# A mamba block and a mixture of experts on one core: the order of the first four and last six sequences written out by instance, and blank rows stored in long runs

## The reference, cut to what matters

```python
# layer 1, for each sequence
xn = layernorm(layernorm(x)) * norm_w + norm_b
x_in, z = split(xn @ in_proj_w.T)                  # 256 channels each
u = silu(conv4(x_in) + conv_b)                     # dense convolution over time, 4 taps
delta_s, B, C = split(u @ x_proj_w.T)              # 1, 16 and 16 columns
delta = softplus(delta_s @ dt_w.T + dt_b)
h[t] = h[t-1] * exp(-delta[t]) + B[t] * u[t]       # recurrence over 512 steps
y[t] = h[t] . C[t]
a = (y * silu(z)) @ out_proj_w.T + residual
x = x + layernorm(a)
# layer 2, over all 8192 tokens
logits = layernorm(x) @ Wr + br                    # 16 experts, the best 2 per token
e_out = layernorm((silu(x W1) * (x W3)) W2) * gamma + beta
x = x + layernorm(w0 * e_out0 + w1 * e_out1)
```

## Time and profile before

| what | us |
|---|---|
| median of 3 runs | 969.74 (968.95 to 969.86) |
| the profiled execution: its own time | 971.61 |
| its span on the core | 969.8 |
| stage 1, to the matmul of the slot columns (L2086) | 0 to 498.8 |
| hand-off, to the first transpose of stage 2 (L2098) | 498.8 to 516.2 |
| stage 2 with the final sums | 516.2 to 969.8 |

### The profile page before, as it was taken

The page is one execution under the profiler, slowest core; times in us unless marked ns, Lnnn a source line. Parts: engine busy times, 40 slices in busy tenths (PEclk is TensorE's granted clock), DMA queues, the critical chain, the costliest instruction groups (busy, mean ns, idle before and its releaser), DMA issues.

```text
span 969.8 us, 26624 instructions
## 1 busy us (share of the span) xinstructions
PE 936.2 (97%) x7189; PEld 829.9 (86%) x7189; DVE 724.0 (75%) x2524; ACT 687.8 (71%) x1355; POOL 619.7 (64%) x814
## 2 busy tenths in 40 slices
PE   8999999999999999998986999999999999999995
PEld 4777877888878877887986999999999999999962
DVE  2379999999999998898832676776777767777747
ACT  3777787777787787774215777777787777877626
POOL 2345677777777777775561666666666666576647
PEclk9999999999999999999997999999999999999998
DMA  4001332221112111111794311111111111111076
GB/s 136 12 12 34 91 96 69 67 78 53 55 56 50 55 40 42 42 22 41 262 310 160 101 44 52 48 52 46 50 50 46 49 50 46 45 52 48 20 274 246
DMA packets 54160, 75.25 MB, mean 78 GB/s; under 512 B 11104, under 2 KB 32866, under 8 KB 53377
## 3 DMA queue, kind: packets, MB, share of 16 engines
q1 hardware_dynamic: 42640, 54.61, 18.5%
q0 software_dynamic: 8672, 16.93, 5.0%
q10 hardware_dynamic: 2704, 2.02, 0.8%
HBM read 47.09 MB, written 27.41 MB: 77 GB/s over the span
## 4 chain that ended last, share of the span: by engine, by line
PE 78%; DVE 7%; POOL 6%; issue 4%; DMA 3%; SPq 1%; ACT 1%; POOLq 0%; DVEq 0%; ACTq 0%
PE pA L2106 11%; PE pR L2106 11%; PE pA L1665 11%; PE pB L2114 6%; PE pY L2114 5%; PE pY L1779 4%; PE pB L1691 3%; PE pB L1825 3%; PE pA L1680 3%; PE pY L1815 3%; POOL chosen_scratch L698 3%; PE pY L1798 2%; PE pY L1747 2%; PE pR L1763 2%; POOL ers L688 1%
## 5 line engine op out<-in xcount | busy, mean ns | idle before, releaser
L698 POOL DMA_INDIRECT chosen_scratch<-yo,got_id x143 | 147.8, 1034 | 94.0 <-issue 88.1
L1026 ACT ACTIVATE stage<-w_sb 128x1024 f32 x143 | 151.2, 1057 | 59.1 <-issue 37.6
L1545 DVE TENSOR_TENSOR hidT<-pR,sil 128x512 f32<-128x512 f32 x143 | 98.9, 692 | 89.7 <-ACT sil L1021 60.9
L612 POOL DMA_INDIRECT slots_scratch<-xrow,send_at x128 | 134.2, 1049 | 34.3 <-issue 30.4
L2106 PE MATMUL pA<-xsT,stage 128*128 128x128 f32 x1144 | 153.0, 277 | 0.4 <-ACT xsT L1010 0.4
L2106 PE MATMUL pR<-xsT,stage 128*128 128x128 f32 x1144 | 152.1, 276 | 0.0
L2106 PEld LDWEIGHTS pA<-xsT,stage 128*128 128x128 f32 x1144 | 140.9, 194 | 0.7 <-ACT xsT L1010 0.7
L2106 PEld LDWEIGHTS pR<-xsT,stage 128*128 128x128 f32 x1144 | 140.1, 193 | 0.0
L1665 PE MATMUL pA<-xn,taps 128*128 128x512 f32 x256 | 129.8, 593 | 1.0 <-DVE taps L1062 1.0
L688 POOL TENSOR_TENSOR ers<-eve,neg_half 128x1 f32<-128x1 f32 x143 | 81.3, 569 | 58.1 <-DVE eve L1557 56.8
L1021 ACT ACTIVATE sil<-pA 128x512 f32<-128x512 f32 x143 | 85.3, 596 | 28.2 <-PE pA L2106 26.2
(11 more groups left out here) (233 smaller groups left out, 2099.7 us busy)
## 6 DMA issues: line engine op xcount, KB each, us to landing
got<-slots_scratch SPq DMA_DIRECT2D x143, 65.0 KB, 1.9
w_sb<-chosen_scratch SPq DMA_DIRECT2D x16, 512.0 KB, 5.3
w_sb<-in_w_dram SPq DMA_DIRECT2D x1, 6144.0 KB, 19.1
xin<-in_x_dram SPq DMA_DIRECT2D x16, 256.0 KB, 3.9
xr<-in_x_dram SPq DMA_DIRECT2D x16, 256.0 KB, 3.1
x_scratch<-x SPq DMA_DIRECT2D x16, 256.0 KB, 3.7
w_sb<-in_w_dram SPq DMA_DIRECT2D x4, 1024.0 KB, 7.8
fx<-x_scratch SPq DMA_DIRECT2D x1, 4096.0 KB, 14.5
```

Source lines behind the costliest of these rows:

```text
L612: eng.indirect_dma_start(slots_d, bass.IndirectOffsetOnAxis(ap=send_at[:, s % 2, k, t:t + 1], axis=0), xrow[:, s % 2, k, t, :], None).then ...
L698: eng.indirect_dma_start(chosen_d, bass.IndirectOffsetOnAxis(ap=got_id[:, j % NGOT:j % NGOT + 1], axis=0), yo[:, q, :], None, bounds_check ...
L1026: eng.activation(stage[:, j % NSTAGE, :, :].rearrange("p k f -> p (k f)"), w13_sb[:, bass.ds(e, 1), :, :].rearrange("p o k f -> p (o k f)" ...
L1545: eng.tensor_tensor(hidT[:, p, :], pR[:, p, :], sil[:, p, :], ALU.mult).then_inc(hid_ready, 1)
```

## The change

Two things are changed. All arithmetic and all tiles but one stay.

First, `run_units` gets a first and an end round, and only runs rounds 0 to 2 on POOL, ACT and PE (0 and 1 on DVE). Everything after that is listed call by call on all four engines: the order of sequences 0 to 3 and 10 to 15 is new in it, the rounds between keep the order they had but for small shifts. SP's order stays. The calls are the same ones as before, each exactly once; only some `keep_warm` counts differ (the first `keep_warm(3)` and the wait for `dec1_ready` in sequence 14 move, and the `keep_warm(10)` ahead of the last `rank` becomes `keep_warm(4)`).

Second, the tile `blank` has 16 partitions with eight rows each in place of 128 partitions with one row each, and a store of 128 blank rows is 16 runs of 4160 bytes in place of 128 runs of 520 bytes.

```diff
-def run_units(ns, rounds, unit):
-    for k in range(rounds):
+def run_units(ns, first, end, unit):
+    for k in range(first, end):
         unit([k - j if 0 <= k - j < ns else None for j in range(DEPTH + 1)])
...
-        blank = sb("blank", [P, ROW])
+        blank = sb("blank", [P // 8, 8 * ROW])
...
-            eng.dma_start(slots_d[bass.ds(row, P), :], blank[:, :]).then_inc(tails_stored, 16)
+            eng.dma_start(slots_d[bass.ds(row, P), :].rearrange("(p r) d -> p (r d)", r=8), blank[:, :]).then_inc(tails_stored, 16)
...
-            eng.memset(blank[:, D:D + 1], float(NOWHERE)).then_inc(blank_ready, 1)
+            eng.memset(blank[:, :].rearrange("p (r d) -> p r d", d=ROW)[:, :, D:D + 1], float(NOWHERE)).then_inc(blank_ready, 1)
...
-            run_units(NS, 20, unit)
+            run_units(NS, 0, 3, unit)
+            rstd_1(2)
+            carry(0, 1)
...
-            keep_warm(10)
+            keep_warm(4)
             eng.wait_ge(lg_read, NS + 1)
             rank(L)
```

More of the change, by code:

```diff
@@ new lines, in _ @@
+            fold(3, 1)
+            gather(3, 1)
+            mask(4, 2)
+            mask(4, 4)
+            odd(4)
+            decayed(3)
+            var_1(7)
+            with_diagonal(3)
+            logits(2)
+            largest(2)
+            where(2)
+            diagonal(4)
+            choose(2)
+            gated(3)
+            positions(2)
+            margin(2)
+            shift_1(7)
+            dots(5)
+            stats_1(8)
+            aggr_1(8)
+            attend(3)
+            stats_3(3)
@@ new lines, in _ @@
+            mask(5, 4)
+            odd(5)
+            decayed(4)
+            var_1(8)
+            with_diagonal(4)
+            logits(3)
+            largest(3)
+            diagonal(5)
+            where(3)
+            margin(3)
+            choose(3)
+            gated(4)
+            positions(3)
+            shift_1(8)
+            dots(6)
+            stats_1(9)
+            aggr_1(9)
+            attend(4)
+            stats_3(4)
+            aggr_3(4)
+            scan(5, 0)
+            var_3(4)
@@ new lines, in _ @@
+            var_1(9)
+            with_diagonal(5)
+            logits(4)
+            largest(4)
+            diagonal(6)
+            where(4)
+            margin(4)
+            choose(4)
+            gated(5)
+            positions(4)
+            shift_1(9)
+            stats_1(10)
+            aggr_1(10)
+            dots(7)
+            attend(5)
+            stats_3(5)
+            aggr_3(5)
+            scan(6, 0)
+            var_3(5)
+            scan(6, 1)
+            expand(7, 0)
@@ new lines, in _ @@
+            logits(5)
+            largest(5)
+            diagonal(7)
+            where(5)
+            margin(5)
+            choose(5)
+            gated(6)
+            positions(5)
+            shift_1(10)
+            stats_1(11)
+            aggr_1(11)
+            dots(8)
+            attend(6)
+            stats_3(6)
+            aggr_3(6)
+            scan(7, 0)
+            var_3(6)
+            scan(7, 1)
+            expand(8, 0)
+            residual(6)
+            stats_4(6)
+            aggr_4(6)
@@ new lines, in _ @@
+            mask(13, 2)
+            mask(13, 4)
+            odd(13)
+            decayed(12)
+            with_diagonal(12)
+            logits(11)
+            largest(11)
+            diagonal(13)
+            where(11)
+            margin(11)
+            choose(11)
+            gated(12)
+            positions(11)
+            dots(14)
+            attend(12)
+            stats_3(12)
+            aggr_3(12)
+            scan(13, 0)
+            var_3(12)
+            scan(13, 1)
+            expand(14, 0)
@@ new lines, in _ @@
+            largest(12)
+            with_diagonal(13)
+            where(12)
+            diagonal(14)
+            choose(12)
+            gated(13)
+            positions(12)
+            dots(15)
+            margin(12)
+            attend(13)
+            stats_3(13)
+            aggr_3(13)
+            scan(14, 0)
+            var_3(13)
+            scan(14, 1)
+            expand(15, 0)
+            residual(13)
+            expand(15, 1)
+            stats_4(13)
+            aggr_4(13)
@@ L1391, in _ @@
+            choose(13)
+            gated(14)
+            positions(13)
+            margin(13)
+            attend(14)
+            stats_3(14)
+            aggr_3(14)
+            scan(15, 0)
+            var_3(14)
+            scan(15, 1)
+            residual(14)
             stats_4(14)
```

1821 lines of the change are left out of this document (1766 added, 55 removed).

## The result

The changed kernel takes 974.84 us (median of 5 runs, 973.51 to 975.62) against 969.86 (968.95 to 971.17, 5 runs): ratio 1.0049, 95% interval 1.0035 to 1.0063, so **5 us slower**. Forecast were 8.1 us faster, 957 to 967. Sign and size were wrong. A second set of runs of the same kernel, on another chip, gave 973.31, ratio 1.0042 (1.0025 to 1.0060).

A forecast was written before the change was run, and what follows sets the result against it. PE was taken to set the pace in steady rounds, DVE in the drain, a blank store the hand-off. Gains 1.0 + 2.3 + 4.3 + 0.5 = 8.1 us: median 969.7 to 961.6, range 957 to 967.

The forecast's parts named there:

- Up to 420 PE is full: Sequences 10 to 15, before 420 us: moved steps gain and cost nothing unless they make PE wait; 0 us.
- (2): Rival: the orders bring nothing, new PE waits in first and last rounds eat the 3.3 us; 964.9 us, chance 0.12.
- (4): Rival: both rival (1) and (2) hold, neither stores nor orders gain; 968.8 us, chance 0.05.
- (5): Rival: slower, a blank store's 16 runs go to few DMA engines (two need 28 us); 976 us, chance 0.04.
- Start: Sequences 0 to 3: the wait for xs filled, two PE waits of 0.2 removed; gain 1.0 us.
- (a): At project_out(13): six warming records ahead of it go, next_b(15) goes ahead; gain 0.9 us.
- (b): At project_out(14): warming ahead of it goes, it starts earlier; gain 1.4 us, between 0.5 and 1.9.
- Last rank: End of stage 1: four warming matmuls for ten start it about 1.4 us earlier, POOL's address only 0.43.
- The blank stores: Hand-off: long runs save 3.2 us of DMA work; gain 4.3 us with the rank's 0.4, bounds 0.4 and 6.5.
- rival (1): Stores bring nothing, 16 partitions feed the engines slowly, only the address's 0.4 is left; 965.5 us, chance 0.20.
- Clock: PE's fall to half clock at the hand-off stays, with less of stage 2 in it; gain 0.5 us, 0 to 3.
- rival (3): More than the sum: clock stays up at the hand-off (up to 2.5 more) or at 452; 958.9 us, chance 0.11.

The follow-up runs named there:

- e2: All the new orders with keep_warm(4), blank tile as before; against the kernel before: +3.2 us [1.6, 4.7].
- e7: Kernel before plus a hand-off probe: seven DVE operations, each beside a POOL operation, four shown again with POOL idle; total time not of interest, none given.
- e8: Kernel before without keep_warm(3) ahead of rank(12) and rank(13), and keep_warm(4) for keep_warm(10) ahead of the last rank: -0.4 us [-1.4, 0.7].
- e1: Kernel before with only the blank tile of 16 partitions and its long runs, every order as before: -0.3 us [-1.8, 1.2].
- e14: Kernel before with 4160-byte blank runs, tile over 128 partitions, each pair of stores reading another 16: 4.9 us faster [-6.6, -3.2].
- e9: Kernel before up to the end of sequence 13's recurrence, from there the new order with keep_warm(4), blank tile as before: +8.4 us [5.7, 11.0].
- e17: Kernel before with e14's spread blank tile and e8's removal of warming matmuls: -0.9 us [-3.2, 1.5] against the kernel before.
- e18: The changed kernel with e14's spread blank tile: +4.6 us [2.2, 6.9] against the kernel before.
- e10: Kernel before with the new order from sequence 7 to the end of sequence 13's recurrence, then the old order with keep_warm(10): +14.2 us [12.8, 15.7].
- e11: Kernel before plus two extra POOL tensor_tensor of 128x512 read from SBUF ahead of each carry(s, 4): 49 us slower [47, 51].
- e12: Kernel before plus five POOL memsets of 128x512, which read nothing, ahead of each carry(s, 4): 1.3 us faster [-2.1, -0.4].

## Why the prediction was wrong, step by step

- **"Up to 420 PE is full, so moves there cost and bring nothing unless they make PE wait."** This is the step that failed. The condition was checked for data (every moved step had its inputs), not for the duration of the steps. DVE had 2.1 us free in a round; moved against POOL's reading operations it stood still for 6.9 to 7.7 us in three rounds, and PE, which had no wait from 317 to 404 us, got 2.3 us of listed waits, 1.8 of them for DVE. The orders are worth -3.2 (e2) in place of the +1.0 and +2.3 of the sum; that PE's new waits, the lower clock behind them and POOL's `token(12)` are all of it is likely and not shown. Among the rivals for the orders (2), at nothing, was the nearest and 3 us short; taken whole, (4), with both parts at nothing, was the nearest but for (5), and its 968.8 is 6 short. A rival in which the orders cost several us was missing. The traces of before had the sign of it: a tensor_scalar of DVE at 0.48 that takes 0.17 elsewhere, and a fold of 0.69 at 1.53 in the drain.
  The Trainium skill has the rule, in "SBUF — State Buffer", section "SBUF: two separate sides": DVE and GpSimd share a port pair as an exclusive lock; a DVE operation with two SBUF inputs (against a GpSimd operation that reads SBUF) or in a 2-port mode, or the GpSimd operation, whichever starts first, keeps it for its whole instruction. e7 agrees for two inputs (1.47 for 0.42 us with both in SBUF, 0.42 with one in PSUM or beside a memset). Its copy and its `tensor_scalar`, with one SBUF input, stood still as well; whether they ran in such a mode no trace shows. The prediction read this page for another section and did not apply it.
- **Start, 1.0:** measured 0.2, which can't be told from none. The wait for xs went as said, one for DVE grew from 0.2 to 0.6. The 0.35 us of the trace are no more than that the clock didn't fall at the start: against the old start without such a fall it is a microsecond late at the fifth `project_out`.
- **(a), 0.9:** nothing (0.08). The bound was put at `gated(13)`, but PE's list has `rank(12)` ahead of `project_out(13)`, and that waits for `chosen_b` of DVE. **(b), 1.4:** 0.5 (e8), for the same reason. The warming matmuls stood in a wait. In the whole new order `attend(13)` waits 1.35, `attend(14)` 2.14.
- **Last rank, 1.4, and address, 0.43:** 1.26 and 0.5 in e8. Right by themselves; behind the new order both are later than before, by 1.6 and 2.4.
- **The blank stores, 4.3:** nothing with the tile as changed (e1), 4.9 with the rows spread (e14). The price per engine was right for the spread source (1.75 us of 16 engines for eight stores, 1.5 seen in e14), and wrong for 16 partitions (3.7 in e1, more than the short runs' 3.4; 2.8 in the changed kernel). So for this term rival (1) held: the stores bring nothing, because few partitions feed the engines slowly, as e14 against e1 shows. The mistake was to price a transfer by a queue's average, with no row that reads 16 partitions. The Trainium skill's warning ("SBUF — State Buffer", "Door 1: The DMA port swizzle") was right in sign: by its rate the prediction had an estimated 10.2 us for all 16 stores, and twice e1's 3.7 are 7.4 us of engine time (the one is elapsed time and the other is not, so only the sign can be compared).
- **Clock, 0.5:** at the start of stage 2 it was at half in most traces, as said; where PE was late, as in the changed kernel's, it had fallen before and was back at full by then, worth 2.9 us, as in rival (3), but as the lesser part of a loss. (By its own 2.5 us that rival is 959.1 and not 958.9.)
- **Rival (5)** had nearly the right total, 976, by luck. It wanted 28 us for the 16 stores; in e1, with this tile alone, the last has landed 15.7 us behind the first issue (496.3 to 512.0), and the time is -0.3.

**What stays open.** The slow issue: PE, ACT and SP execute one instruction in 0.7 us at the hand-off. It is in seven of 20 traces: for some 9 us in the changed kernel, e9, e17 and e18, for about half as long in e10, e11 and e12. It is not the long runs (e9 to e12 have the short ones) nor the shorter warming (e10 to e12 have `keep_warm(10)`). Where it is long, the first transpose stands 23.0 to 24.1 behind the address, in place of 16.4 to 21.5 elsewhere; PE's clock is then at full when stage 2 starts, which pays some of it back, and in e12, where it is short, seems to pay for all of it. All of e17's runs lie above e14's, though on another chip, so it seems to come in most executions of that kernel. In the second trace of the changed kernel it is missing. What starts it was not found, and whether a shorter `keep_warm(40)` would hide it was not tried. The parts alone sum to +2.9 and the whole was +4.8 and +4.1: what the parts leave, 1 to 2 us, may be this or noise.

Open too is the order's own loss: a list that keeps DVE's steps off POOL's was not found, and POOL's order, with `token(12)` behind `carry(13, 8)`, was not tried alone.

The fastest kernel was e14, which is the kernel before with the blank tile spread: 965.03 us.

## What to carry to other kernels

When steps of DVE and POOL are reordered, list which of them read SBUF only and see what stands beside what: a step keeps its duration only beside the neighbours it had. Before DMAs are given longer runs, count the partitions that they read together; with the stores spread over all of them eight rows a run paid, with all from the same 16 they did not. And a warming matmul is no cost while the step behind it in the list waits for another engine.

## What was not expected of the hardware

- Two POOL operations of 1.3 to 1.6 us a round, for which nobody waits, cost 49 us in all (e11); five memsets, together 2.7 us, cost nothing (e12).
- A `tensor_scalar` of 128x4 f32 took 1.15 us beside POOL, 0.17 alone (e7): the lock's price is that of the other engine's operation, however small one's own.
- PE, ACT and SP at one instruction in 0.7 us, with no wait in the profile, for up to 9 us (above).
